# Moving a copy of transposed probabilities ahead of the second exponentials in each attention slot

## The reference

```python
x = x + _L0_xattn_ref(_layernorm(x), ctx, ...)   # cosine similarities
x = x + _L0_ffn_ref(_layernorm(x), ...)          # all eight experts, gated
x = x + _L1_xattn_ref(...); x = x + _L1_ffn_ref(...)   # one head; top 2 of 8, relu
x = x + _L2_xattn_ref(...); x = x + _L2_ffn_ref(...)   # 16 heads; top 2, silu gate, shared expert
x = x + _L3_xattn_ref(...); x = x + _L3_ffn_ref(...)   # 16 heads; top 2, relu, biases
```

```python
attn = softmax(einsum('bhqd,bhkd->bhqk', q, k) * SCALE)
out  = einsum('bhqk,bhkd->bhqd', attn, v)
```

## Time and profile before

| | |
|---|---|
| median of three runs | 2332.05 us |
| runs | 2325.49 to 2333.19 us |
| profiled execution, whole | 2331.31 us |
| its span, first to last instruction | 2329.2 us |
| mean granted TensorE clock | 0.879 |
| TensorE (PE) busy | 1905.1 us, 82% |
| VectorE (DVE) busy | 1250.2 us, 54% |
| ScalarE (ACT) busy | 1053.2 us, 45% |
| GpSimd (POOL) busy | 888.3 us, 38% |

### The profile page before, as it was taken

The page is one execution under the profiler, slowest core; times in us unless marked ns, Lnnn a source line. Parts: engine busy times, 40 slices in busy tenths (PEclk is TensorE's granted clock), DMA queues, the critical chain, the costliest instruction groups (busy, mean ns, idle before and its releaser), DMA issues.

```text
span 2329.2 us, 35764 instructions
## 1 busy us (share of the span) xinstructions
PE 1905.1 (82%) x11048; PEld 1365.5 (59%) x11048; DVE 1250.2 (54%) x3395; ACT 1053.2 (45%) x3404; POOL 888.3 (38%) x891
## 2 busy tenths in 40 slices
PE   3999999989989987778788899788899787786662
PEld 1565555555556876555566777565778444563452
DVE  2447567466565322455556667565667545464532
ACT  1444444434434223666555445555445455574321
POOL 1666776676766212133232111431210432205333
PEclk7999999999999998888887999788899657796686
DMA  4505106204100975331004463102654103541583
GB/s 135 193 5 186 68 13 207 98 13 120 67 10 18 319 243 186 112 94 50 14 22 157 154 250 109 30 21 104 208 196 158 36 22 106 137 107 34 150 239 95
DMA packets 162552, 261.34 MB, mean 112 GB/s; under 512 B 23564, under 2 KB 96590, under 8 KB 161998
## 3 DMA queue, kind: packets, MB, share of 16 engines
q1 hardware_dynamic: 137406, 228.10, 30.3%
q0 software_dynamic: 12288, 25.19, 3.6%
q10 hardware_dynamic: 12672, 5.77, 0.9%
HBM read 195.03 MB, written 82.00 MB: 119 GB/s over the span
## 4 chain that ended last, share of the span: by engine, by line
PE 50%; DVE 14%; ACT 11%; issue 10%; another core or an unknown queue 7%; POOL 4%; DMA 1%; SPq 1%; ACTq 0%; DVEq 0%; POOLq 0%
PE up L917 9%; PE Y L1002 7%; PE up L984 6%; ACT prob L1171 5%; PE Y L926 4%; PE B L810 3%; PE A L802 3%; PE D L820 2%; PE up L989 2%; ACT probT L1177 2%; PE up L802 2%; DVE nmax L1369 1%; ACT kbd L1159 1%; POOL hid L1851 1%
## 5 line engine op out<-in xcount | busy, mean ns | idle before, releaser
L1851 POOL TENSOR_TENSOR hid<-tg,uc 112x512 f32<-112x512 f32 x192 | 249.0, 1298 | 182.3 <-ACT uc L1226 142.8
L1177 ACT ACTIVATE probT<-B 128x512 f32<-128x512 f32 x256 | 156.4, 611 | 336.3 <-PE B L810 252.5
L1796 POOL DMA_INDIRECT list<-xn,pos x192 | 190.6, 993 | 300.9 <-DVE pos L1511 249.5
L926 PEld LDWEIGHTS Y<-wd,hid 112*128 112x128 f32 x1536 | 201.9, 194 | 142.1 <-issue 110.1
L1585 DVE SCALAR_TENSOR_TENSOR tg<-tg,up 112x512 f32<-112x512 f32 x192 | 131.4, 685 | 223.5 <-ACT tg L1222 222.2
L810 PE MATMUL B<-const,prob 128*128 128x128 f32 x1024 | 195.1, 323 | 61.9 <-ACT probT L1177 48.3
L810 PEld LDWEIGHTS B<-const,prob 128*128 128x128 f32 x1024 | 138.6, 166 | 173.5 <-issue 164.1
L926 PE MATMUL Y<-wd,hid 112*128 112x128 f32 x1536 | 208.8, 279 | 32.2 <-DVE ytmp L1595 18.9
L1222 ACT ACTIVATE tg<-up 112x512 f32<-112x512 f32 x192 | 114.8, 598 | 258.6 <-PE up L917 219.1
L1692 DVE COPY xsT<-Y 128x128 f32<-128x128 f32 x248 | 71.6, 289 | 274.2 <-PE Y L954 193.2
L1171 ACT ACTIVATE prob<-up,nmax 128x128 f32<-128x128 f32 x596 | 212.7, 389 | 0.0
(11 more groups left out here) (236 smaller groups left out, 4029.8 us busy)
## 6 DMA issues: line engine op xcount, KB each, us to landing
w_tile<-wt SPq DMA_DIRECT2D x45, 768.0 KB
list<-w_tile SPq DMA_DIRECT2D x21, 1536.0 KB, 13.2
w_tile<-wt SPq DMA_DIRECT2D x45, 512.0 KB
w_tile<-wt SPq DMA_DIRECT2D x50, 321.0 KB
wg<-list SPq DMA_DIRECT2D x248, 64.0 KB
wd<-wt SPq DMA_DIRECT2D x17, 768.0 KB
list<-wu SPq DMA_DIRECT2D x160, 64.0 KB
wd<-wt SPq DMA_DIRECT2D x17, 512.0 KB
```

The costliest lines, as they stand in the source:

```text
L926: mm = pe.matmul(Y4[:, t, :], hid[0:rows, i % HRING, t * P:(t + 1) * P], wd[0:rows, i, :], start=(c == 0 and t == 0), stop=(c == PER_UNIT[ ...
L1177: act.activation(probT[:, (2 * r + i) % 4, :, :], B4[:, :, :], ACT.Copy).then_inc(probT_done.sem, 1)
L1796: pool.indirect_dma_start(out=list_to(K, g)[:, :], in_=xn2[:, t, :], in_offset=None, out_offset=bass.IndirectOffsetOnAxis(ap=pos[:, g, s, ...
L1851: pool.tensor_tensor(hid[0:rows, i % HRING, :], tg[0:rows, i % 2, :], uc[0:rows, i % 2, :], ALU.mult).then_inc(hid_ready.sem, 1)
```

## The change

In ScalarE's `slot`, for slots whose `first` half holds a turn, the copy of the second quad's transposed probabilities moves from behind the whole half to behind its first turn, and the exponentials of the slot's second quad move from behind the first turn to behind the whole half. Slots with an empty `first` keep their order. No other engine's queue changes, and no instruction is added or removed.

```diff
                 tile_turns(first[:1])
+                if first and last:
+                    evacuate_probs(*last, rl, 1)
+                tile_turns(first[1:])
                 if now:
                     exponentials(*now, r, 1)
-                tile_turns(first[1:])
-                if first and last:
-                    evacuate_probs(*last, rl, 1)
                 if r == 4 and ahead:
                     read_queries(*ahead)
                 tile_turns(second)
```

## The result

The changed kernel takes 2352.83 us (median of four runs, 2351.13 to 2363.15) against 2329.36 us (2325.49 to 2333.19) for the kernel before, measured again beside it. The ratio is 1.0096, with a 95% interval of 1.0065 to 1.0128: about 22 us slower. The forecast was 2352, that is 20 us above the median before of 2332; the same kernel's median beside the change is 2329.36, so the near hit of the absolute time is closer than the sum deserves: 20 forecast stand against 22 (15 to 30) measured.

What follows compares the result with a forecast made beforehand. TensorE, busy 82%, was taken to bound the kernel, so its waits count. Layer 1 -12, shared -4.5, routed +19.4, layer 3 +5.3, late completions +12 sum to +20.2 on 2332: 2352 us, range 2344 to 2361.

Steps and rivals of the forecast that it cites:

- Part 3: Routed layer-2 slots 42 to 55, 74 to 87: copy ahead of the second turn's tanh delays TensorE's next turn, +19.4 us.
- Rival 4: Routed layer-2 stretches: new waits also lower TensorE's granted clock, adding 13 us for 2365, or 2377 at 0.89; chance 0.15.
- Part 5: Slots with TensorE signals late while POOL issues indirect DMAs: steps now queue behind them, +12 us taken, bounds 0 and 17.7.
- Part 1: Layer-1 slots 1 to 21: copy 1.37 us earlier frees TensorE's waits for it, 12 us gained, bounds 8 to 14.
- last condition of being wrong: Layer-1 slots: prediction fails if TensorE's freed waits return at another instruction (tile rows' copies, VectorE); no size given.
- Part 2: Shared-tile slots 25 to 41, 57 to 73: about even, sooner weigh_values against later exponentials, -4.5 us, bounds -6 to +4.
- Part 4: Layer-3 slots 105 to 118: copy ahead of the second turn's relu delays the next turn's product, +5.3 us.
- Rival 1: Two-turn slots: something unmoved holds TensorE anyway, so the late tanh costs nothing and gains stay, 2315 us; chance 0.10.
- rival 2: Whole kernel: all hidden, or gain and cost cancel, with no late completions, about 2332 us; chance 0.12.
- rival 3: Whole kernel: only the firm sum of +8.2 us, late completions ending at POOL's times, 2340 us; chance 0.15.

Runs made afterwards that it cites:

- run 11: New order only in one-turn slots, with read_queries ahead of the second exponentials for r = 4, against the kernel before: 2326.62 us, ratio 0.9963.
- run 12: run 10 with read_queries ahead of the second exponentials in one-turn slots with r = 4; 2330.34 us, ratio 0.9982 to the kernel before.
- run 1: New order only in slots whose first half holds two turns, against the kernel before: 2372.11 us, ratio 1.0165.
- run 4: Kernel before with, in two-turn slots only, the copy moved ahead of the second turn and the exponentials left ahead: 2376.46 us, ratio 1.0157.
- run 2: New order only in slots whose first half holds one turn, against the kernel before: 2319.06 us, ratio 0.9933.
- run 6: New order only in one-turn slots from 24 on (shared tiles), against the kernel before: 2322.28 us, ratio 0.9978.
- run 7: New order only in slots 43, 47, 55, 75, 79, 87 (late completions), against the kernel before: 2338.22 us, ratio 1.0057.
- run 8: New order only in slots 42, 48 to 51, 74, 80 to 83, against the kernel before: 2343.66 us, ratio 1.0076.
- run 3: Kernel before with, in two-turn slots only, the exponentials moved last and the copy left behind the second turn: 2334.49 us, ratio 1.0006.
- run 5: New order only in one-turn slots below 24 (layer-1 tiles), against the kernel before: 2317.14 us, ratio 0.9966.
- run 9: Changed kernel with TensorE's second-quad transposes moved behind the first turn instead of the whole first half; 2316.77 us, ratio 0.9922 to the kernel before.
- run 10: run 9 with ScalarE's exponentials between copy and second turn in two-turn slots; 2325.43 us, ratio 0.9964 to the kernel before.

## Why the prediction came out right, point by point

One profile's stretch wanders by some us where nothing is changed: slots 88 to 104, which no kernel changes, took from 132.8 to 143.3. So each stretch is read from all profiles at once, one for each kernel: the mean of those in which its slots have the new order against the mean of those with the order before. (The ends are the starts of ScalarE's first copy in the bounding slots; shared and routed stand for the tiles.)

| slots | order before | new order | difference | forecast |
|---|---|---|---|---|
| 1 to 23, layer 1 | 169.8 (7 kernels) | 164.1 (7) | -5.7 | -12 |
| 24 to 41, shared | 168.3 (7) | 162.1 (5) | -6.2 | -1 for both |
| 57 to 73, shared | 157.0 (7) | 157.1 (5) | +0.1 | |
| 42 to 55, routed | 191.1 (5) | 208.7 (3) | +17.6 | +27.1 for both |
| 74 to 87, routed | 191.7 (5) | 206.4 (3) | +14.7 | |
| 105 to 118, layer 3 | 141.3 (7) | 145.2 (3) | +3.9 | +6.0 |

The 12 us of late completions in the forecast are dealt out here by its list (12 of 17.7 of each entry). Runs 11 and 12, which move `read_queries` as well, count as new order in the first row only (and run 11 as the order before in layer 3 and the routed tiles); a kernel that has neither order in a stretch is left out of its row. The differences sum to +24.4, beside +22.4 by the ratio and +20.2 forecast.

**Part 3: the mechanism was right and its size nearly so.** The two routed stretches lost 32.3 where 27.1 was forecast. In the same means TensorE's busy time, for the same products, grew by 6.5 (42 to 55: 174.2 to 176.9; 74 to 87: 172.8 to 176.6), and its idle time by 25.8. So the waits, late completions included, cost about what was forecast for them, and what was missing is time at the lower clock, a term that the sum had at nothing. By period, from before to after: slots 49, 50, 81, 82 +1.22 to +1.23 (forecast 1.15), the four with r = 5 +0.98 to +1.00 (0.9), the four with r = 6 +0.10 to +0.11 (0), the two of r = 4 that follow no late slot, 52 and 84, +0.55 and +0.56 (0.28). Slots 51 and 83 lost 1.70: there TensorE's down product waits for VectorE's copy at the slot's front, 1.40 now and 1.03 before, as VectorE is behind too. The term that was mis-sized most plainly is slots 42 and 74, +3.15 and +3.77 instead of 2.0 and 1.15. TensorE's lines of slot 42, changed kernel:

```profile
1261.41 1.91 PE L984 MATMUL up<-xsT,wd 128*128 128x128 f32 x8
...
1264.39 0.60 PE L810 MATMUL B<-const,prob 128*128 128x128 f32 x4
...
1266.98 1.73 PE L984 MATMUL up<-xsT,w_tile 128*128 128x128 f32 x8 [1.88 <-DVE tg L1681]
```

The product that waits starts at +2.59, where the sum put it. But it then takes 1.73, where the same one took 1.06 before. The windows of slots 42 and 74 (columns as the earlier trace rows), first changed, then before:

```profile
1259.77:1276.10 16.33, 13.15 (x82) 11.16 (x82) 8.84 (x28) 5.66 (x22) 1.24 (x2) 0.79 0.70 265
1635.04:1651.46 16.42, 13.24 (x82) 11.25 (x82) 8.84 (x28) 5.66 (x21) 1.24 (x2) 0.79 0.92 352
```

```profile
1269.15:1282.33 13.18, 11.79 (x82) 9.84 (x82) 8.75 (x28) 5.78 (x21) 1.25 (x2) 0.87 0.84 317
1624.86:1637.51 12.65, 10.46 (x82) 8.31 (x82) 8.75 (x28) 5.67 (x21) 1.25 (x2) 1.00 1.03 401
```

The same 82 records of TensorE are busy 1.4 and 2.8 us longer, at a granted clock of 0.79. Where the profiles of such kernels show these slots at 1.00, the price is the plain one: slot 74 of run 1 took 13.82 and slot 42 of run 4 took 13.83, against 12.65 in the old order at 1.00, +1.17 and +1.18. So the 2.0 of slot 42 was too high for the plain price: it came from the profile before, in which that slot stands at 0.87 and C's product at +0.55; where the old order has the slot at 1.00 (runs 2, 6 and 7), it stands at +1.41 or +1.42, as in slot 74. In run 8 they took 16.65 and 15.03, at 0.80 and 0.89: +6.4 together where the sum had 3.2. In run 1, slot 42 took 16.65, and in run 4, slot 74 took 15.04. With 1.1 more in 51 and 83 the ten clean slots of run 8 cost 12.3 + 3.2 + 1.1 = 16.6; run 8's routed stretches stand 16.5 above the mean of the old order, and its time +18.

**Rival 4 (clock as well)** is thus right in its mechanism and half as large as priced, 6.5 and not 13: over the whole stretch, where before had 0.95, the changed kernel has 0.94 (and 0.93 in slots 74 to 87, where before had 0.96).

```profile
1260.00:1469.00 209.00, 178.19 (x1321) 151.31 (x1321) 124.35 (x322) 87.75 (x313) 29.94 (x35) 0.94 0.48 164
```

The Trainium skill's TensorE: Matmul & The Clock Gate, section What's actually happening, lets the gate follow how busy TensorE has been. The traces agree in direction only: in the profiles of the changed kernel and of runs 1, 4 and 8, slots 42 and 74 have the same wait of 1.88, and the product behind it took 1.40 to 1.73 in six of the eight cases and 1.13 in two (slot 42 of run 4, slot 74 of run 1). In the changed kernel the lower level was also there ahead of the wait: the first G product took 1.91 in both slots (0.50 granted), and the clock was back at 1.00 by the wait. In slot 42 the kernel before has such a product too, in slot 74 it took 1.07. So not all of slot 74's price is the wait's, and what decides between the cases stays open.

**Part 5, the late completions, was right in the routed slots as far as can be told.** Slot 47 of the changed kernel, against the earlier trace rows:

```profile
1345.68 0.60 PE L810 MATMUL B<-const,prob 128*128 128x128 f32 x4
...
1351.82 0.60 ACT L1177 ACTIVATE probT<-B 128x512 f32<-128x512 f32 x1 [9.46 <-remote]
1352.31 0.59 ACT L1247 ACTIVATE tg<-up 128x512 f32<-128x512 f32 x1
...
1353.77 2.04 PE L984 MATMUL up<-xsT,wd 128*128 128x128 f32 x8 [6.48 <-DVE tg L1681]
```

Copy at +6.14 (before +6.11), and tanh B behind it at +6.63 in place of +3.19; C at +8.09 in place of +4.65. The slot itself grew by 1.63 only, and slot 48 by 3.33. The six slots 43, 47, 55, 75, 79, 87 grew by 12.9 in the changed kernel's profile, but 44 and 76 right behind late ones shrank by 1.4 and 1.2. The full list had 13.7 for the six (11.4, and 2.3 for 43 and 75 at the plain rate), the forecast 10.0. Run 7 took 13 longer (7 to 19), and its two routed stretches stand 9.3 above the mean of the old order, so both sums fit. Slots 31, 39 and 63 were over-priced: +2.3 together and not 5.2.

**Part 1 was half right: waits went away at the copy, fewer than forecast, and a part of them came back at another instruction.** TensorE's waits in the stretch, before (to be read with the earlier trace rows) and changed:

```profile
PE Y L954 <- DMA wg<-list: 5.2, 2, 3.6
PE D L820 <- ACT probT L1177: 3.8, 4, 1.2
```

```profile
PE Y L954 <- DMA wg<-list: 9.1, 2, 7.0
PE B L810 <- ACT probT L1177: 6.1, 3, 4.6
PE D L820 <- ACT probT L1177: 2.2, 1, 2.2
```

The one that grew most is the wait for the load of a tile's rows in slot 16. The queue of SP and what it stands behind, changed kernel:

```profile
1035.56 1.16 PE L782 MATMUL up<-wv,ctxT 97*128 97x128 f32 x8
...
1041.76 0.34 SPq L680 DMA_DIRECT2D ctxT<-in_ctxT  x1
1041.76 0.60 ACT L1164 ACTIVATE va<-up 128x512 f32<-128x512 f32 x1 [4.47 <-remote]
...
1043.18 0.36 SPq L633 DMA_DIRECT2D wg<-list  x1
...
1045.09 0.44 PE L954 MATMUL Y<-const,wg 128*128 128x128 f32 x1 [7.04 <-DMA wg<-list]
```

SP issues the load of the context (L680) when the value product (L782) is done with the old one, and that signal arrives late, 6.2 us after the product's start (4.8 to 6.6 in all profiles, whatever the order); the rows' load stands behind it. Before:

```profile
1045.37 0.45 PE L954 MATMUL Y<-const,wg 128*128 128x128 f32 x1 [3.59 <-DMA wg<-list]
```

Counted from slot 1's first copy (929.89 before, 933.53 now), this transpose stands at 115.48 before and at 111.56 now: of 7.4 us that TensorE had gained by then, 3.9 are kept and 3.5 are waited away. In the means of the table's profiles TensorE's idle time straight ahead of L810 and L820 fell by 8.4 in slots 1 to 23, that ahead of L954 grew by 3.0, and the whole shrank by 5.7. The even slots gained in sum what was forecast (-0.61 to -1.53 each, -7.5 together, in 2, 6, 8, 10, 14, 16, 18). So the step that failed was adding up freed waits slot by slot as gained, without asking what TensorE would then wait for that does not come sooner by as much. The prediction named that possibility as its last condition of being wrong.

**Part 2: its first stretch gained 6 where 1 was taken for both together.** In slot 34 the scores come at +2.68 (forecast 2.75), in slot 36 the router's products at +3.26, 0.6 later and not 1.0. But the TensorE busy time of the same 791 records fell as well, 134.4 to 128.4 from before to after. In the table's means it fell by 3.8 (132.5 to 128.7) and the idle time by 2.4, so more than half of the gain of 6.2 is clock and not the freed waits. Before and after:

```profile
1099.33:1269.15 169.82, 134.39 (x791) 98.44 (x791) 96.19 (x255) 89.79 (x361) 49.19 (x54) 0.82 0.14 45
```

```profile
1099.66:1259.77 160.11, 128.39 (x791) 94.18 (x791) 95.98 (x255) 90.35 (x360) 47.06 (x52) 0.86 0.14 46
```

One product shows it: in slot 37 the key product (L777) took 2.08 us before and 1.12 after, each after the same wait of 2.6.

```profile
1229.95 2.08 PE L777 MATMUL up<-ctxT,wk 97*128 97x512 f32 x2 [2.59 <-DVE aoT L1391]
```

```profile
1223.84 1.12 PE L777 MATMUL up<-ctxT,wk 97*128 97x512 f32 x2 [2.60 <-DVE aoT L1391]
```

In this stretch the profiles of kernels with the order before have granted clocks of 0.82, 0.84, 0.85, 0.84, 0.82, 0.86 and 0.84 (before, runs 1, 3, 4, 5, 7, 8), those with the new one 0.86, 0.88, 0.85, 0.86, 0.88, 0.86 and 0.86 (changed, runs 2, 6, 9 to 12). In the second shared stretch the changed kernel has 0.82 as before, and the length hardly moves. Whether the new order raises the clock in the first, or something that comes with it, was not tried; by time, run 6 gives -5 (-11 to +1) for both stretches.

**Part 4** was priced some 2 too high: slots 106, 113, 114 and 115 lost 0.49 each, not 0.6 to 0.9.

So the total is right because the largest term was right, and by luck in the rest, where three terms missed in opposite ways: too little gained in layer 1 (6), more in the shared stretches than was taken (5), time at the lower clock in the routed ones (5 to 7). Rival 1 falls with TensorE's 40.5 us of waiting for L1681; rivals 2 and 3 (+0 and +8) lie below the interval of the measured ratio, +15 to +30 us, and rival 4 (+33) lies above it.

## What to carry to other kernels

On an in-order queue a step that starts no earlier than its producer allows gains nothing by being placed earlier, and holds back whatever it is put ahead of (runs 1 and 4). Ask first whether the producer is already issued at that point of its own queue. If it isn't, move producer and consumer together (run 9), or leave both. A reorder that applies to several kinds of slots is several changes; the version that keeps only those that gain costs one condition (run 2).

## What the runs showed of the hardware that was not expected

- The price of one and the same delay on TensorE hung on the granted clock: a product later by 1.17 in slot 74 cost 1.17 us where the slot was at 1.00 (run 1) and 2.38 where it was at 0.89 (run 8). In the changed kernel (0.79) the slot took 3.77 longer, of which 1.3 are the two products ahead of the wait, at 1.91 and 1.54 in place of 1.07 and 1.06. A wait of 1 us in slots 49 to 51 had no such effect.
- TensorE's clock level can differ between profiles at the same instruction: the key product of slot 37 took 2.08 us (granted clock 0.50 during it) and 1.12 us (1.00), behind the same wait of 2.6.
- TensorE's signals come up to 6.1 us after the instruction's start while POOL issues a run of indirect DMAs (slot 47: transposes at 1345.68, copy at 1351.82; eight indirect DMAs from 1340.30 to 1350.27). In slots 47 and 79 of the kernel before and the changed one the copy starts 1.46 to 1.55 after the end of the last of them, in slots 43 and 75 of the changed one 1.14 to 1.16 before it. That both fall together is seen; that the one causes the other was not tried, and stays open.
